# A two-block vision tower on one core: the opening in another order, and a layer norm's steps spread over the units of attention

## What is computed

```python
h = patch_embedding(x) + position            # 36 patches of 768 values, a class token
h = h + attention0(layernorm(h))             # 16 heads of 64, causal, softmax
h = h + ffn0(layernorm(h))                   # 256 -> 1024 -> 256, piecewise-linear GELU, rounded to 1/256
h = h + attention1(layernorm(h))             # 16 heads of 64, no causal mask
h = h + experts(layernorm(h))                # 8 experts 256 -> 1024 -> 256, gates from a k-th largest logit
def layernorm(x): return (x - mean(x)) / sqrt(var(x) + 1e-5)     # over the 256 features
```

## Time and profile before

| what | us |
|---|---|
| median of 3 runs (1036.73, 1036.98, 1046.01) | 1036.98 |
| the profiled execution | 1043.69 |
| its span | 1041.9 |
| TensorE's mean granted clock in it, share of full | 0.965 |

### The profile page before, as it was taken

The page is one execution under the profiler, slowest core; times in us unless marked ns, Lnnn a source line. Parts: engine busy times, 40 slices in busy tenths (PEclk is TensorE's granted clock), DMA queues, the critical chain, the costliest instruction groups (busy, mean ns, idle before and its releaser), DMA issues.

```text
span 1041.9 us, 18653 instructions
## 1 busy us (share of the span) xinstructions
PE 966.6 (93%) x7166; PEld 890.4 (85%) x7166; DVE 572.0 (55%) x1243; ACT 543.1 (52%) x1569; POOL 158.4 (15%) x174
## 2 busy tenths in 40 slices
PE   4699999998889989999998989999999999999998
PEld 4587878876868778879786989899999999999998
DVE  4736465555599664564636476754544444444442
ACT  3365454645366455454534553555555555556552
POOL 0152122211000022122211000052111111111111
PEclk9899999989699999999987699999999999999999
DMA  7230000001100200000001111111111111100001
GB/s 265 81 123 1 2 2 1 2 2 41 41 1 1 81 28 15 1 1 2 2 1 41 41 41 42 41 42 41 42 41 42 41 42 42 42 1 2 1 13 36
DMA packets 8637, 34.48 MB, mean 33 GB/s; under 512 B 610, under 2 KB 5090, under 8 KB 5220
## 3 DMA queue, kind: packets, MB, share of 16 engines
q1 hardware_dynamic: 8548, 33.28, 8.8%
HBM read 32.06 MB, written 1.22 MB: 32 GB/s over the span
## 4 chain that ended last, share of the span: by engine, by line
issue 30%; PE 23%; DVE 6%; POOL 5%; ACT 2%; POOLq 0%; DVEq 0%; ACTq 0%
PE D L531 8%; PE O L531 7%; POOL h L333 4%; PE O L655 2%; PE T L641 1%; PE S L630 1%; DVE wslot L1054 1%; DVE hid L1376 1%; PE S L531 1%; POOL h L345 1%; PE T L568 1%; DVE probsT L1156 1%; PE T L576 1%; PE S L624 1%; PE O L748 1%
## 5 line engine op out<-in xcount | busy, mean ns | idle before, releaser
L531 PE MATMUL O<-hid,wslot 128*128 128x300 f32 (+3 forms) x1680 | 245.5, 305 | 2.0 <-DVE hid L1165 2.0
L1376 DVE TENSOR_TENSOR hid<-work,hid 128x300 fp32r<-128x300 f32 (+1 forms) x256 | 137.1, 555 | 199.3 <-ACT hid L1011 197.1
L531 PE MATMUL D<-xn,wslot 128*128 128x300 f32 (+3 forms) x1368 | 230.5, 315 | 13.1 <-DVE h L1063 8.3
L531 PEld LDWEIGHTS O<-hid,wslot 128*128 128x128 f32 x1680 | 237.3, 192 | 3.3 <-DVE hid L1165 2.3
L531 PEld LDWEIGHTS D<-xn,wslot 128*128 128x128 f32 x1368 | 205.6, 196 | 18.5 <-issue 9.3
L1007 ACT ACTIVATE work<-D,prm 128x300 f32<-128x300 f32 (+1 forms) x128 | 66.7, 521 | 187.7 <-PE D L531 187.4
L906 ACT ACTIVATE probs<-S,negmax 111x111 f32<-111x111 f32 (+1 forms) x352 | 117.5, 359 | 79.6 <-DVE negmax L1141 79.2
L510 POOL TENSOR_TENSOR probs<-probs,rsum 111x444 f32<-111x444 f32 (+1 forms) x88 | 79.5, 904 | 413.2 <-DVE rsum L1149 413.2
L531 PE MATMUL S<-xn,wslot 128*128 128x300 f32 (+3 forms) x864 | 137.0, 307 | 0.0
L531 PEld LDWEIGHTS S<-xn,wslot 128*128 128x128 f32 x864 | 127.2, 194 | 0.3
L1141 DVE TENSOR_REDUCE negmax<-S 111x4 f32<-111x444 f32 (+1 forms) x88 | 52.5, 599 | 94.8 <-PE S L630 94.8
(11 more groups left out here) (152 smaller groups left out, 1178.5 us busy)
## 6 DMA issues: line engine op xcount, KB each, us to landing
raw<-in_moe SPq DMA_DIRECT2D x16, 1024.0 KB, 4.8
raw<-in_attn SPq DMA_DIRECT2D x8, 1024.0 KB, 4.9
work<-in_x SPq DMA_DIRECT2D x2, 1008.0 KB, 8.3
raw<-in_ffn SPq DMA_DIRECT2D x1, 1024.0 KB, 4.7
w2f<-in_ffn SPq DMA_DIRECT2D x1, 1024.0 KB, 8.3
raw<-in_x SPq DMA_DIRECT2D x1, 1008.0 KB, 6.8
out<-h SPq DMA_DIRECT2D x3, 300.0 KB, 2.9
raw<-in_w_lin SPq DMA_DIRECT2D x1, 768.0 KB, 4.2
```

The source lines that it names most:

```text
L531: mm = pe.matmul(psum, a, b, start=(first and k == 0), stop=(k == 3 * n - 1))
L1376: nc.vector.tensor_tensor(moe_hid(s, 1), moe_g(s)[:, 0:w], moe_hid(s, 0).bitcast(F32), ALU.subtract).then_inc(m_hid, 1)
```

## The change

In the opening, the first chunk of patches is loaded and split in two halves of 3 of its 6 feature rows, and TensorE starts when the first half is split. VectorE makes the low parts of pieces 0 and 1 ahead of the small tables, and the masks right behind the low part of piece 2. The norm of chunk 0 comes one product earlier. VectorE, not GpSimd, splits piece 6 (NSTART is 7).

In attention, VectorE adds the two feature halves of h at the end of unit u - 1 (`add_halves`), so that `mean` is one matmul, placed between the value projection and the second transposes of unit u. Centring and square are in unit u too. VectorE adds the two halves of the squares in unit u + 1 (`add_squares`), and `variance` is one matmul at the end of that unit. `finish` becomes `newton` (three operations instead of four, ahead of `low_out`) and `apply` (behind it) in unit u + 2. The four norms outside attention (LN_WHOLE) keep both matmuls. `prepare` loses the masks and the clearing, and moves to the end of unit 4 of attention 0; the bias row is loaded to another buffer. The functions `low_part`, `low_quarter`, `set_h` and `center` are moved up unchanged.

```diff
+LN_WHOLE = ((0, 0), (1, NC - 1), (2, 0), (3, NC - 1))
...
-        b1row = probs[0:BL + 1, :, :].rearrange("p s n -> p (s n)")[:, 0:FF]
+        b1row = ffs[0:BL + 1, :, :].rearrange("p s n -> p (s n)")[:, 0:FF]
...
-        NSTART = FIRST_W + 1
+        NSTART = FIRST_W + 2
...
+        def halves(n, c):
+            return sum((n, k) not in LN_WHOLE for k in range(c + 1))
...
-                if 0 < i < FIRST_W:
+                if i == 1:
+                    n = KF // 2
+                    sp.dma_start(x0_half(dst, 0).rearrange("p (k n) -> p k n", k=n), src[:, 0:n, :]).then_inc(x0_in, 16)
+                    dst, src = x0_half(dst, 1).rearrange("p (k n) -> p k n", k=n), src[:, n:KF, :]
+                elif 0 < i < FIRST_W:
...
-            def embed(c):
...
-                pe.wait_ge(*piece_split(1 + c))
-                for dc in range(KD):
-                    if c >= 1:
-                        pe.wait_ge(h_set, KD * (c - 1) + dc + 1)
...
+                if dc == 0:
+                    pe.wait_ge(*((x0_low, 1) if c == 0 else piece_split(1 + c)))
+                if c >= 1:
+                    pe.wait_ge(h_set, KD * (c - 1) + dc + 1)
...
+                               KF, emb_mm,
+                               between=(lambda: pe.wait_ge(*piece_split(1))) if c == 0 and dc == 0 else None)
...
             def mean(n, c):
                 a, w = CHUNKS[c]
-                pe.wait_ge(NORMED[n], KD * (c + 1))
+                whole = (n, c) in LN_WHOLE
+                pe.wait_ge(*((NORMED[n], KD * (c + 1)) if whole else (ln_sum[n], halves(n, c))))
                 if before(n, c):
                     n0, c0 = before(n, c)
                     pe.wait_ge(ln_out[n0], c0 + 1)
+                if not whole:
+                    pe.matmul(BLN[:, 0:w], mean_w[:, :], sq[:, 0, 0:w], start=True,
+                              stop=True).then_inc(ln_mean[n], 1)
+                    return
...
             def variance(n, c):
...
+                whole = (n, c) in LN_WHOLE
+                pe.wait_ge(*((ln_sq[n], c + 1) if whole else (ln_sum2[n], halves(n, c))))
+                if not whole:
+                    pe.matmul(BLN[:, 0:w], mean_w[:, :], sq[:, 0, 0:w], start=True,
+                              stop=True).then_inc(ln_var[n], 1)
+                    return
...
                     if u < NUNIT:
                         project_v(u)
+                    if ln_due(l, u):
+                        mean(*ln_due(l, u))
                     if 0 <= u - 1 < NUNIT:
...
                     if ln_due(l, u - 1):
                         variance(*ln_due(l, u - 1))
-                    if ln_due(l, u):
-                        mean(*ln_due(l, u))
...
             pe.wait_ge(*piece_split(0))
-            embed(0)
-            embed(1)
+            embed(0, 0)
+            embed(0, 1)
+            embed(1, 0)
             pe.wait_ge(consts, 1)
             mean(0, 0)
-            embed(2)
+            embed(1, 1)
             variance(0, 0)
-            embed(3)
+            for c in (2, 3):
+                for dc in range(KD):
+                    embed(c, dc)
             attention(0, 0)
...
-            for i in range(FIRST_W):
-                high_part(i)
+            high_part(0)
+            act.wait_ge(x0_in, 16)
+            nc.scalar.activation(x0_half(piece_place(1)[0], 0), x0_half(piece_raw(1), 0), ACT.Copy).then_inc(x0_high, 1)
+            landed(act, 1)
+            nc.scalar.activation(x0_half(piece_place(1)[0], 1), x0_half(piece_raw(1), 1), ACT.Copy).then_inc(high_ready, 1)
+            high_part(2)
             nc.scalar.preload_act_table_set("natural_log_exp_and_others")
+            high_part(3)
...
                         exps(2 * u)
                         exps(2 * u + 1)
-                    if ln_due(l, u - 1):
-                        square(*ln_due(l, u - 1))
                     n = 0 if due is not None else 1
...
                     for i in blocks[n:]:
                         move_q(i)
+                    if ln_due(l, u):
+                        square(*ln_due(l, u))
...
             square(0, 0)
+            high_part(4)
+            inv_root(0, 0)
             high_part(FIRST_W)
-            inv_root(0, 0)
             high_part(FIRST_W + 1)
             high_part(FIRST_W + 2)
             attention(0)
...
+            def add_halves(n, c):
+                a, w = CHUNKS[c]
+                dve.wait_ge((h_set, h_attn[0], h_ff, h_attn[1])[n], KD * (c + 1))
+                n0, c0 = before(n, c)
+                dve.wait_ge(ln_var[n0], c0 + 1)
+                nc.vector.tensor_tensor(sq[:, 0, 0:w], h[:, 0, a:a + w], h[:, 1, a:a + w],
+                                        ALU.add).then_inc(ln_sum[n], 1)
+            def add_squares(n, c):
+                w = CHUNKS[c][1]
+                dve.wait_ge(ln_sq[n], c + 1)
+                nc.vector.tensor_tensor(sq[:, 0, 0:w], sq[:, 0, 0:w], sq[:, 1, 0:w],
+                                        ALU.add).then_inc(ln_sum2[n], 1)
+            def newton(n, c):
+                w = CHUNKS[c][1]
+                dve.wait_ge(ln_rs[n], c + 1)
+                r, t = rs[:, 0:w], rt[:, 0:w]
+                link(nc.vector.scalar_tensor_tensor(t, BLN[:, 0:w], EPS, r, ALU.add, ALU.mult))
+                link(nc.vector.scalar_tensor_tensor(t, t, -0.5, r, ALU.mult, ALU.mult))
+                return tick(nc.vector.scalar_tensor_tensor(r, t, 1.5, r, ALU.add, ALU.mult))
+            def apply(n, c, root):
+                a, w = CHUNKS[c]
+                dve.wait_ge(dve_line, root)
+                x2 = xc[:, :, 0:w]
+                rb = rs[:, 0:w].rearrange("p (a n) -> p a n", a=1).to_broadcast([P, KD, w])
+                link(nc.vector.tensor_tensor(x2, x2, rb, ALU.mult))
+                link(nc.vector.tensor_copy(xn[:, 0, :, a:a + w], x2))
+                nc.vector.tensor_tensor(xn[:, 1, :, a:a + w], x2, xn[:, 0, :, a:a + w].bitcast(F32),
+                                        ALU.subtract).then_inc(ln_out[n], 1)
+            def finish(n, c):
+                apply(n, c, newton(n, c))
+            def low_x0(k):
+                dve.wait_ge(*((high_ready, 2) if k else (x0_high, 1)))
+                high, low = piece_place(1)
+                nc.vector.tensor_tensor(x0_half(low, k), x0_half(piece_raw(1), k), x0_half(high.bitcast(F32), k),
+                                        ALU.subtract).then_inc(start_split if k else x0_low, 1)
+            low_part(0)
+            low_x0(0)
+            low_x0(1)
...
-            def finish(n, c):
-                a, w = CHUNKS[c]
-                dve.wait_ge(ln_rs[n], c + 1)
-                r, t = rs[:, 0:w], rt[:, 0:w]
-                link(nc.vector.tensor_tensor(t, r, r, ALU.mult))
-                link(nc.vector.scalar_tensor_tensor(t, BLN[:, 0:w], EPS, t, ALU.add, ALU.mult))
-                link(nc.vector.tensor_scalar(t, t, -0.5, 1.5, ALU.mult, ALU.add))
-                link(nc.vector.tensor_tensor(r, t, r, ALU.mult))
...
-            low_part(0)
-            low_part(1)
+            low_part(2)
+            dve.wait_ge(mats_in, 64)
+            nc.vector.tensor_copy(masku[:, :], maskf[:, 2, :]).then_inc(masks, 1)
+            for l in range(2):
+                for i in range(QH):
+                    ins = nc.vector.tensor_copy(maskb[:, l, i, :], maskf[:, l, :])
+            ins.then_inc(masks, 1)
             dve.wait_ge(params, 3)
-            for c in range(NC):
-                low_part(c + 2)
-                set_h(c)
-                if c == 2:
-                    finish(0, 0)
-                if c == 1:
-                    center(0, 0)
+            set_h(0)
+            low_part(3)
+            center(0, 0)
+            set_h(1)
+            low_part(4)
+            finish(0, 0)
+            set_h(2)
+            low_part(FIRST_W)
+            set_h(3)
+            low_part(FIRST_W + 1)
+            def clear_gaps():
+                dve.wait_ge(emb_mm, KD * NC)
+                nc.vector.memset(
...
             def prepare():
-                dve.wait_ge(mats_in, 64)
                 dve.wait_ge(gt_pick, 1)
                 for row in (0, DH):
                     ins = nc.vector.tensor_copy(pick[row:row + E, :], ident[row:row + E, row:row + E])
...
                     ins.then_inc(h_attn[l], 1)
                 if l == 0:
-                    prepare()
+                    clear_gaps()
                 else:
                     for k in range(SPLITS):
                         low_quarter(FIRST_W + 8, k)
+                add_halves(*ln_due(l, 0))
...
                     if u < NUNIT:
                         row_max(2 * u + 1)
-                    if ln_due(l, u - 1):
-                        center(*ln_due(l, u - 1))
...
                     if due is not None:
                         add_out(due, 0)
+                    if ln_due(l, u):
+                        center(*ln_due(l, u))
+                    if ln_due(l, u - 1) and ln_due(l, u - 1) not in LN_WHOLE:
```

(9 more changed lines are left out.)

54 lines of the change are left out of this document (27 added, 27 removed).

## The result

The changed kernel takes 1010.19 us (median of 4 runs, 1008.74 to 1012.38) against 1039.12 for the kernel before beside it (1036.73 to 1046.01): 0.971 of its time, 95% interval 0.966 to 0.977. It is faster by more than the 1% that the prediction set as its bound. The profiled execution takes 1012.38, its span is 1010.6 and its granted clock 0.972 of full (before: 1043.69, 1041.9 and 0.965). Two later executions of the kernel before were far slower, 1198.5 and 2346.0 us, and are in no ratio.

What follows compares the result with a forecast made beforehand. TensorE, busy 93% of the span, was taken as the bound. Terms -10.8 - 12.4 - 1.5 - 9.5 - 3 + 2.6 + 0.5 = -34.1 us, from the median 1037.0, gave 1003 us; range for 8 in 10: 993 to 1018.

Steps and rivals of the forecast that it cites:

- Two of its signs: Signs of being right: waits before the second transposes below 0.8 us, and unit 20 no shorter.
- One sign of being wrong: In units 3, 9, 12 and 18: row maxima later than 1.5 us behind their scores.
- The opening: Before attention 0: TensorE starts 3.6 us earlier and piece 5's low part ends near 34.6; 10.8 us won, bounds 7 to 12.
- the collision: Opening: GpSimd's split of piece 6 stretches VectorE's L1091 from 0.86 to 5.09 us; moving the split wins 4.2 us.
- The matmuls: Twelve norms in attention: one matmul fewer for mean and variance each, 12.4 us; mean covering a wait for VectorE's copy, 1.5.
- The stall behind each finish: Eight waits before second transposes, 13.2 us, from late row maxima behind `finish`: 9.5 go, 3.7 stay; bounds 4 and 12.
- The clock at unit 18: Both attentions: lower clock behind unit 18's wait costs about 3 us each; one of two falls goes, 3 us, bounds 0 to 6.
- The fourth rival: Both clock falls go and nothing is late: 41 us won, 996 us; chance 0.15.
- The tails: End of each attention: centring delays the last unit's row maxima; 1.3 us lost an attention, 2.6 together.
- `prepare`: Unit 4 of attention 0: some 3 us of VectorE work in a gap of about 2.5, costing 0.5 us.
- The base: Terms applied to the median 1037.0, 6.7 us below the profiled 1043.7, giving 1002.9 rather than 1009.6 us.
- The prediction's 0.4 us: Attention: GpSimd's 0.93 us product may hold a VectorE operation with two SBUF inputs in the Newton step some 0.4 us.

Runs made afterwards that it cites:

- the kernel with both matmuls: The changed kernel without the added feature and square halves, so mean and variance in attention have two matmuls each again: 1020.7 us, ratio 0.977.
- the kernel with only the opening: The new opening and shorter Newton step, with attention's norms at their old places and with both matmuls: 1027.7 us, 0.983 of the kernel before.
- The combined kernels: Three kernels: the change with `prepare` in unit 13, late quarter splits and early piece 5, then two variants moving ScalarE's second conversion: 1002.7, 1000.0 and 998.1 us.
- the kernel with Newton at the end: The changed kernel with the three Newton operations moved back behind `low_out`, so all of `finish` stands there: 1016.2 us, ratio 0.973.
- the third combined kernel: Change plus three edits (`prepare`, quarter splits, piece 5), ScalarE's second conversion behind the last unit, Newton behind `low_out` in the last step: 998.1 us, ratio 0.956.
- quarters late: The changed kernel with VectorE's quarter splits of the last weights moved from units 20 and 21 to after the last unit: 1007.6 us, ratio 0.966.
- the first two combined: The change with `prepare` in unit 13, late quarter splits and early piece 5: 1002.7 us; then with ScalarE's second conversion one unit later: 1000.0 us.
- prepare in 13: The changed kernel with `prepare` at the end of unit 13 of attention 0 instead of unit 4: 1008.1 us, ratio 0.967.
- piece 5 early: The changed kernel with piece 5's low part behind the first norm's Newton step, and that norm's `apply` behind `set_h` of chunk 2: 1004.2 us, ratio 0.964.
- the change, twice: The changed kernel and its unaltered repeat beside later experiments: 1010.2 us, ratio 0.971, and 1010.8 us, ratio 0.969.
- piece 6 on GpSimd: The changed kernel with piece 6 split by GpSimd again instead of VectorE: 1014.0 us, ratio 0.971.
- the repeat of the change: The changed kernel run once more, unaltered, beside three later experiments: 1010.8 us, ratio 0.969.

## Why the prediction was right, and where its terms were off

Forecast were 34.1 us less, made against the profiled execution; the profiled executions differ by 31.3, and 0.971 of 1039.1 is 29 less. The range and the sign held. Two of its signs did not: waits before the second transposes stay above 0.8 us (0.86, 0.85, 1.25), and unit 20 got shorter. One sign of being wrong was just touched, row maxima 1.51 us behind their scores in unit 3 of attention 1. No rival came whole. Term by term:

**The opening: 10.8 forecast, 9.4 measured.** The walk held to about 0.1 us at each point that it named (9.5, 34.6, 41.65). It missed the clock: its own wait from 39 to 41.8 stood in the text, and it was priced as a wait alone. In this execution the clock fell behind it. It need not: with the same wait, the kernel with both matmuls shows (weight loads)

```profile
41.35 1.85 PEld L551 LDWEIGHTS D<-xn,wslot 128*128 128x128 f32 x12 [2.90 <-ACT work L935]
43.17 0.96 PEld L551 LDWEIGHTS O<-xn,wslot 128*128 128x128 f32 x6
```

and its scores at 46.86, 11.2 us earlier than before. So the term is 9.4 to 11.2, by the clock. Of its parts only the collision was taken back alone, 3.5 us; that TensorE starts 3.5 us earlier stands in the traces (13.03 to 9.51), but neither the halved first chunk nor the earlier norm was tested by itself.

**The matmuls: 12.4 + 1.5 forecast, 12.5 measured** (5.9 and 6.6, the clear part of the comparison with both matmuls). The main term was right; how much of the 1.5 is real can't be read apart from it.

**The stall behind each finish: 9.5 forecast.** Of the eight waits named, 13.2 us, three are left: 0.86 and 0.85 in unit 18 and 1.25 in unit 3 of attention 1, 3.0 together where 3.7 was forecast; 0.78 in unit 5 (`prepare`) and 0.96 and 0.97 in the tails are new. The mechanism was right, a program order that delays the next unit, and the size too: the shorter step gives 1.5 us an attention without the clock (4.7 - 3.2), the new order 3.6 (2.9 + 0.7 for `prepare`, and 3.6), 10.2 in all.

**The clock at unit 18: 3 forecast, 6.4 measured.** Both falls went, 3.2 us each, where one was counted. They are gone in the kernel with only the opening already, where the wait was still 1.62 us. That one was counted and two went is not the mechanism's merit: the prediction had no rule for it, and none was found. The fourth rival, both falls gone and nothing late, was half met: the falls were gone, but the tails were late and the clock fell elsewhere.

**The tails: 2.6 forecast for both, 4.0 measured.** This is the mis-sized term: "the 1.1 us won by the mean are lost and 0.2 more, 1.3 an attention". The new order alone cost 1.9 and 2.0 (16.52 to 18.44, 16.53 to 18.57), of which the added halves won 1.3 and 1.5 back. Unit 20 did get shorter (5.96 to 5.02 us), against the forecast, and what stands behind it got longer. The tail after, weight loads from unit 20 to the last projection of attention 0:

```profile
228.64 0.46 PEld L672 LDWEIGHTS T<-ident,probs 111*111 111x111 f32 x4 [0.96 <-issue]
...
230.63 0.77 PEld L686 LDWEIGHTS O<-probsT,vbuf 111*64 111x64 f32 x16 [1.52 <-DVE probsT L1231]
...
234.54 0.28 PEld L672 LDWEIGHTS T<-ident,probs 74*74 74x74 f32 x4 [1.92 <-issue]
...
237.42 5.19 PEld L551 LDWEIGHTS O<-hid,wslot 128*128 128x128 f32 x24 [1.29 <-DVE hid L1240]
```

The waits shown add up to 5.7 us in 9; before, the long ones there were 0.89, 1.52 and 1.17, 3.6 together. The text looked at one reason, what VectorE does ahead of the row maxima of the last unit. The combined kernels show what the tail can give back, 2.6 us an attention: the quarter splits (1.1), ScalarE's conversion (1.4) and the Newton step ahead of the last `low_out` (0.1). The first two stand in the kernel before as well, so how the new order came to cost 1.9 us, by the centring in front of the row maxima or otherwise, was not separated.

**`prepare`: 0.5 forecast, 0.69 measured.**

**Counted at nothing, and not nothing: the rest, 3.4 us slower.** Its program is the same but for the shorter Newton step, and the time follows the clock. Windows after, and of the kernel with Newton at the end, over the same 60 us of the work behind attention 1 (busy us and count of each engine, granted clock, DMA share, GB/s):

```profile
527.60:567.60 40.00, 37.52 (x208) 36.82 (x208) 15.28 (x36) 16.67 (x31) 0.00 (x0) 0.67 0.09 32
567.60:587.60 20.00, 17.87 (x109) 17.50 (x110) 12.71 (x57) 9.14 (x20) 0.00 (x0) 0.83 0.00 1
```

```profile
535.76:575.76 40.00, 35.65 (x213) 34.96 (x214) 18.73 (x48) 19.21 (x34) 0.00 (x0) 0.74 0.08 28
575.76:595.76 20.00, 18.68 (x135) 17.95 (x134) 15.63 (x68) 9.90 (x24) 0.00 (x0) 1.00 0.11 37
```

The second does 348 matmuls in the 60 us and the first 317. Over all the profiles the length of this stretch goes with the clock lost in it (10 us times one minus the granted clock, summed over its whole 10 us slices), except that below 10.7 it falls no further:

| clock lost, us | the rest, us | kernels |
|---|---|---|
| 8.5 | 477.6 | the third combined kernel |
| 10.3 to 10.7 | 477.3 to 477.8 | Newton at the end; quarters late; the first two combined |
| 13.3 to 13.7 | 479.6 to 480.2 | before; both matmuls; prepare in 13; piece 5 early |
| 15.3 | 481.7 | only the opening |
| 16.6 | 482.8 to 483.0 | the change, twice; piece 6 on GpSimd |

So it is not the change's work that slows this part: by the falls that it meets, an execution spends from 477.3 to 483.0 us here. The plainest case is `prepare` in unit 13. Its program is the change's from unit 14 on, only 2.1 us earlier, and it takes 480.2 us. Why the change met the long one in both its profiles stays open. With piece 6 on GpSimd the same program starts 5.2 us later and is as long, with piece 5 early it starts 3.9 us earlier and takes 480.1; one profile of each can't tell a rule from chance.

**The base.** Of the 7.2 us between forecast and median, 2.8 come from the terms (1.4 less in the opening and 3.4 lost in the rest, against 1.3 more in the attentions and 0.8 in the feed-forward part). The other 4.4 come from the step "the median is 6.7 lower", taken from three runs of which two agreed; the profiled execution after is only 2.2 above its median. The kernel before had medians of 1039.1 to 1046.7 in five comparisons. Its other 32 executions beside the experiments fall in two groups with nothing between: 10 take 1036.9 to 1041.6 us at a granted clock of 0.971 to 0.977, and 22 take 1044.5 to 1051.0 at 0.960 to 0.967. The profiled one (1043.7 at 0.965) is nearest the second, the base of 1037.0 is of the first. The groups lie some 7 us apart, and the two falls at unit 18 are worth 6.4: if the first group lacks these falls, then the step down to 1037 and the term of the clock counted the same time twice. That is not shown, since no profile of the first group is on record. 1043.7 - 34.1 = 1009.6 is within 0.6 us of the median measured, but partly by luck, since the terms are 2.8 us too large.

## What to carry to other kernels

Where engines hold their programs in a fixed order, what stands at the end of a unit delays the next unit: put it into a gap that the engine already has, but look at the last unit by itself, where no work of a next unit covers a delay. Trace a late start back to the one transfer that all of it hangs on, and move the instruction that frees its buffer. Compare stages at like clock rather than totals, take as base the execution that the terms were read from, and look whether the executions of one kernel fall in groups.

## What was unexpected of the hardware

**The clock falls at waits that look alike.** It fell behind waits of 1.98 us and 2.89 us (the change), and did not behind 1.62, behind 2.54, or behind 2.90 in the kernel with both matmuls. Behind the same wait of 3.13 us, before the fourth projection, it fell in the repeat of the change and did not with `prepare` in unit 13, whose program is the same up to there. One fall cost 1.5 us in the opening and 3.2 at unit 18, and the length of a wait alone doesn't foretell it.

**GpSimd and VectorE hold each other, whichever is second.** VectorE's operations with two SBUF inputs take 5.09 instead of 0.86 us, 5.59 instead of 2.28, 4.83 instead of 0.48 and 0.94 instead of 0.51 beside a GpSimd operation that had started first: each ends 0.4 to 2.1 us after it, not far from its own length alone. The prediction's 0.4 us was the last of these. It goes the other way too. GpSimd's split of one tile takes 4.55 us by itself (the opening of the change, above), and 4.94 and 5.31 where it started 0.50 and 0.82 us before the end of such a VectorE operation (L1137 with piece 6 on GpSimd, L1073 with piece 5 early): it is 0.39 and 0.76 us longer. The Trainium skill, SBUF — State Buffer, section SBUF: two separate sides, states that the pair of ports is locked for a whole instruction, and the one that comes second is blocked until the first ends. The four VectorE times and the two GpSimd times agree.
